# Two adaptive-norm transformer layers on one core: layer 1's modulation and residual placed elsewhere, layer 0's gates applied at the combination, PE's mixture programs written out with constant waits

## The chip, the cores and the metric

The kernel runs on one core of one Trainium2 chip, as one launch. Its engines are called here as the profile calls them: PE (matmul, with PEld for its weight loads), DVE (vector), ACT (activation), POOL (GpSimd) and SP (which mostly issues transfers). The metric is device microseconds of the whole execution, lower is better. A span is the time from the first to the last instruction of the program in the profiled execution.

## The reference, cut to what matters

The input is x of 2 batches x 512 tokens x 256 channels. Each of two layers does attention and a mixture of experts, both with a modulated norm ahead and a gate at the residual:

```
mod = (silu(c) @ wmod).reshape(2, 6, 1, 256)
sa, ca, ga, sb, cb, gb = (mod[:, i] for i in range(6))
ga, gb = [(2 * (g >= 0) - 1) * maximum(abs(g), 0.25) for g in (ga, gb)]
h = layernorm(x) * (1 + ca) + sa
x = x + ga * attention(h)                  # 16 heads of 16, causal
h = layernorm(x) * (1 + cb) + sb
x = x + gb * mixture(h)
# layer 0: 8 experts, the best 2 by score, hidden 176
#   comb = softmax(top 2); y_e = silu(h @ w1_e + b1_e) @ w2_e + b2_e
#   mixture(h) = sum_e comb_e * y_e
# layer 1: 16 experts, the best 4, 2 x 256 hidden
#   t = h * rsqrt(mean(h * h) + eps) * norm_w; G = softmax(top 4)
#   a, b = min(even, 7), clip(odd, -7, 7) of (t @ w1_e + b1_e)
#   y_e = (a * sigmoid(1.702 * a) * (b + 1)) @ w2_e + b2_e
#   mixture(h) = h + sum_e G_e * y_e
```

## The kernel before, in words

All 1024 tokens stay in SBUF as 8 tiles of 128 (`x`, `tok`). Each engine has a program of its own (the functions under `nc.Block()`), written out by hand in order, and semaphores tie them together. What stands first in an engine's program goes first, so an instruction that waits holds up everything behind it on its engine.

**Routing.** Behind the second norm of a layer PE turns the tokens batch by batch (`turn_batch(l, 2, b)`, L1310 is its transposes) and multiplies them with the gate weights (L1510). DVE takes the best scores (L1110 to L1127), subtracts the largest (L1131), ACT takes the exponent (L787), and DVE makes the gates of it (L1134 to L1136). PE counts with triangular and all-one matrices which token stands where among an expert's tokens (L1520 to L1527). DVE works out each token's slot and, per tile, tables of zeros and ones (L1177, L1181, L1185); ACT multiplies one of them with the gates (L798). With these tables PE places token numbers and weights into slots of 128 (L1535, `placed_ps`). DVE reads the token list (L1196 to L1199) and the expert of each slot tile, kept in `te` (L1200 to L1203).

**Layer 1's modulation** is computed within layer 0: PE makes its columns (L1285, `modulation_columns(1)`) and its rows (L1296, `modulation_rows(1)`) behind the gate matmuls of both batches. ACT copies the rows out (`move_modulation`, L700), DVE shapes them after the token list.

**Mixture.** Layer 0 has 23 slot tiles, layer 1 has 47. POOL gathers a tile's tokens from DRAM (L635). PE goes in steps: step s transposes tile s (`pe_x`, L1549), loads two expert numbers from `te` into registers (`experts_of`), does the first expert layer of tile s-1 (`pe_h`: bias L1564, weights L1567), transposes the hidden values of s-2 (`pe_hT`, L1576) and does the second layer of s-3 (`pe_y`: bias L1585, weights L1588). On PE, ACT and DVE the first 7 steps and the last 3 are written out; those between are a loop of four steps (`Fori`, `UNROLL`), whose waits compare semaphores with registers. ACT scales each result by its slot's weight while it evicts it (L836). Layer 0 stores the results to DRAM, and POOL gathers each token's two results back (L665, 16 gathers, with the inverse root of layer 1's first norm, L570, put in between them). Layer 1 adds them into DRAM rows (L644).

**Combination and residual.** `combine(l, b)` adds the two results of a pair of tiles (L926), multiplies by the modulation gate (L927) and adds to x (L929). For layer 0 it runs once behind the mixture (first batch) and once within layer 1 behind the first attention fills (second batch). In layer 1 the token itself is part of the mixture's result: POOL multiplies `tok` by the gate and adds it to x (L625, L629), behind the second norm, while DVE does the routing.

Of the kernel before, what the change touches and what calls it, by code (L numbers as in the profile page):

```python
# [10 lines left out]
P = 128  # L11
D = 256
KD = D // P
B = 2
S = 512
T = B * S
NT = T // P
# [48 lines left out]
def build_kernel(nc, dram, out):  # L66
    with ExitStack() as ctx:
# [140 lines left out]
        def weighed_tile(l):  # L208

            n = NT * TOPK[l]  # L210
            return at_tile[:, 0:n * 2 * MT[l]].rearrange("p (n a c) -> p n a c", n=n, a=2)
# [86 lines left out]
        h_added = sem("h_added")  # L298
# [261 lines left out]
        def _(pool):  # L560
# [12 lines left out]
            for l in range(2):  # L573
# [98 lines left out]
        def _(act):  # L672
# [30 lines left out]
            for l in range(2):  # L703
# [80 lines left out]
                if l == 0:  # L784
                    move_modulation(1)
# [5 lines left out]
                act.wait_ge(gate_ready, l + 1)  # L791
                act.wait_ge(brows_ready, 48 * (l + 1))
                for t in range(NT):
                    act.wait_ge(tile_of, NT * l + t + 1)
# [36 lines left out]
                def act_y(ii, off):  # L831
                    i, r, rnd = tile_at(ii, off)
                    act.wait_ge(y_ps[l], i + 1)
                    if not (isinstance(i, int) and i < 4):
                        act.wait_ge((y_kept, y_summed)[l][r], 16 * rnd)
                    nc.scalar.activation(yt[:, r, :], ps[6 + off % 2][:, 0:D], ACT.Copy,  # L836
                                         scale=weight[:, bass.ds(i, 1)]).then_inc(y_sb[l], 1)
# [23 lines left out]
        def _(dve):  # L861
# [57 lines left out]
            def combine(l, b):  # L919

                for m in (2 * b, 2 * b + 1):
                    rng = slice(2 * m, 2 * m + 2)
                    dve.wait_ge((acc_loaded, sums_loaded)[l][m], 64 if l == 0 else 32)
                    if l == 1:
                        dve.wait_ge(h_added, b + 1)
                    link(nc.vector.tensor_tensor(acc_in[:, 0, rng, :], acc_in[:, 0, rng, :], acc_in[:, 1, rng, :], ALU.add))  # L926
# [5 lines left out]
            for l in range(2):  # L932
# [173 lines left out]
                for b in range(B):  # L1106
# [19 lines left out]
                    with nc.allow_low_precision(reason="zeros and ones"):  # L1126
# [9 lines left out]
                nc.vector.tensor_tensor(gate[:, :, 0:K], gk, grec[:, :].unsqueeze(2).broadcast_to([P, NT, K]),  # L1136
                                        ALU.mult).then_inc(gate_ready, 1)
# [18 lines left out]
                for b in range(B):  # L1156
# [16 lines left out]
                    if l == 0 and b == 1:  # L1173
                        count(nc.vector.tensor_copy(slot_u[:, :], slotf[:, 0:NT * K]))
# [541 lines left out]
```

## Time and profile before

| what | value |
|---|---|
| median of 3 runs (lowest to highest) | 662.5 us (659.71 to 666.78) |
| the profiled execution | 663.1 us |
| its span | 661.3 us |
| busy share of the span: PE, DVE, ACT, POOL | 78%, 54%, 37%, 36% |
| mean granted clock of PE | 0.88 |

The kernel's stages lie one behind the other in the span: layer 0's attention up to about 150 us, its routing to 190, its mixture to 262, then its combination, layer 1's attention from 283, its routing from 443 to 473, its mixture to 642 and the end. An engine's share of the whole span says little, as each stage has a limit of its own; one stage is read from its timeline. "Idle before" names the time an engine stood still ahead of an instruction and what released it; "issue" means that the engine waited for nothing that the profile shows but its own sequencer.

### The profile page before, as it was taken

What the parts mean: (1) busy time and instruction counts of PE and PEld (TensorE: products, weight loads), DVE (VectorE), ACT (ScalarE), POOL (GpSimd) and SP (SyncE); (2) the same over time, 40 slices, a digit from 0 to 9 for tenths busy, and PEclk for the clock granted to TensorE, in tenths of its full rate; (3) what the DMA queues carried; (4) which work ended last, traced back from release to release, by engine and by line L of the source; (5) the groups of instructions that cost most, each with busy time, mean ns of one, the idle gap of its engine ahead of it and who ended that gap; (6) DMA issues with size and microseconds to landing.
All of it is one profiled execution on the core that took longest, in us unless ns stands there. A gap on an engine that the chain in (4) does not pass through costs nothing.

```text
span 661.3 us, 10115 instructions
## 1 busy us (share of the span) xinstructions
PE 515.3 (78%) x3124; PEld 336.8 (51%) x3125; DVE 355.3 (54%) x832; ACT 247.3 (37%) x546; POOL 239.0 (36%) x236
## 2 busy tenths in 40 slices
PE   3978889977759997073989898743599999999960
PEld 3444446546447775042545454533556666666640
DVE  3539777446452332347686863577544444444425
ACT  1425546642122322040256546422334444444430
POOL 2213130010033320733121700064247777777650
PEclk9989989998757999576999989965789999999995
DMA  8588160352035331328863633380125444444445
GB/s 284 79 102 106 34 128 5 134 235 82 0 97 168 104 96 56 95 61 106 129 88 51 176 129 131 141 308 2 32 49 81 79 79 79 79 75 80 67 42 196
DMA packets 34858, 67.21 MB, mean 102 GB/s; under 512 B 6628, under 2 KB 27572, under 8 KB 33928
## 3 DMA queue, kind: packets, MB, share of 16 engines
q0 software_dynamic: 14496, 31.08, 26.5%
q1 hardware_dynamic: 20040, 35.64, 17.7%
q8 instruction: 21, 0.34, 0.2%
q14 instruction: 13, 0.11, 0.1%
q10 hardware_dynamic: 288, 0.05, 0.0%
HBM read 38.92 MB, written 14.96 MB: 81 GB/s over the span
## 4 chain that ended last, share of the span: by engine, by line
PE 63%; DVE 14%; DMA 10%; ACT 4%; issue 4%; POOL 4%; SPq 0%; POOLq 0%; DVEq 0%; ACTq 0%
PE bank L1567 15%; PE bank L1588 9%; PE bank L1437 5%; PE bank L1407 4%; PE bank L1387 4%; DVE mx L1029 4%; DMA big<-parts 3%; PE bank L1549 3%; DMA big<-mT 3%; PE bank L1564 2%; PE bank L1576 2%; PE bank L1535 2%; PE bank L1363 2%; POOL ptm L665 2%; PE bank L1310 2%
## 5 line engine op out<-in xcount | busy, mean ns | idle before, releaser
L1029 DVE TENSOR_REDUCE mx<-bank 128x4 f32<-128x512 f32 (+2 forms) x96 | 98.0, 1041 | 39.2 <-PE bank L1390 38.7
L761 ACT ACTIVATE ptm<-bank 128x512 f32<-128x512 f32 x160 | 92.4, 597 | 58.5 <-PE bank L1410 55.8
L1567 PE MATMUL bank<-big,ptm 128*128 x280 | 112.0, 524 | 0.0
L635 POOL DMA_INDIRECT ptm<-token_rows,token x70 | 69.0, 985 | 101.6 <-DVE token L1199 51.3
L644 POOL DMA_INDIRECT sums<-ptm,token x47 | 74.4, 1584 | 31.1 <-ACT ptm L836 29.6
L430 POOL DMA_DIRECT2D big<-parts x72 | 38.8, 546 | 119.0 <-DVE parts L958 58.4
L1387 PE MATMUL bank<-big 96*128 96x128 bf16 (+3 forms) x256 | 64.0, 316 | 22.6 <-DMA big<-parts 15.8
L1407 PE MATMUL bank<-big 98*128 98x128 bf16 (+3 forms) x256 | 67.7, 309 | 11.0 <-DMA big<-mT 6.3
L1588 PE MATMUL bank<-big,ptm 128*128 (+1 forms) x280 | 73.0, 382 | 0.0
L1241 DVE TENSOR_SCALAR tok<-bank 128x256 f32<-128x256 f32 x47 | 20.0, 425 | 85.2 <-PE bank L1567 85.2
L1567 PEld LDWEIGHTS bank<-big,ptm 128*128 128x128 f32 x280 | 51.6, 198 | 26.3 <-issue 23.5
L1390 PE MATMUL bank<-constb 128*128 128x128 bf16 x256 | 52.5, 231 | 0.0
L820 ACT ACTIVATE ctxden<-tok 128x256 f32<-128x256 f32 x47 | 19.6, 417 | 87.8 <-DVE tok L1241 87.8
L1588 PEld LDWEIGHTS bank<-big,ptm 128*128 128x128 f32 (+1 forms) x280 | 48.1, 192 | 4.9
L1410 PE MATMUL bank<-constb 128*128 128x128 bf16 x256 | 49.0, 224 | 0.0
L570 POOL TENSOR_TENSOR rstd<-vareps,neghalf 128x4 f32<-128x4 f32 x8 | 8.6, 1077 | 108.9 <-DVE vareps L906 108.9
L1407 PEld LDWEIGHTS bank<-big 98*128 98x128 bf16 x256 | 25.5, 100 | 42.0 <-ACT ptm L761 17.7
L1387 PEld LDWEIGHTS bank<-big 96*128 96x128 bf16 x256 | 26.5, 104 | 39.3 <-issue 28.7
L836 ACT ACTIVATE ptm<-bank,weight 128x256 f32<-128x256 f32 x70 | 33.2, 475 | 28.2 <-PE bank L1588 24.6
L1437 PE MATMUL bank<-ptm,big 128*32 128x128 f32 (+3 forms) x512 | 41.9, 447 | 1.4 <-ACT ptm L761 1.4
L1549 PE MATMUL bank<-consts,ptm 128*128 128x128 f32 x140 | 29.0, 291 | 11.9 <-DMA ptm<-token_rows,token 11.9
L1310 PE MATMUL bank<-consts,tok 128*128 128x128 f32 x80 | 14.2, 336 | 28.5 <-DVE tok L915 24.2
(173 smaller groups left out, 835.2 us busy)
## 6 DMA issues: line engine op xcount, KB each, us to landing
big<-parts POOLq DMA_DIRECT2D x72, 128.0 KB, 5.9
big<-in_moe_dram SPq DMA_DIRECT2D x1, 6144.0 KB, 19.4
big<-in_moe_dram POOLq DMA_DIRECT2D x1, 4096.0 KB, 15.3
big<-in_moe_dram SPq DMA_DIRECT2D x1, 3456.0 KB, 11.3
big<-parts SPq DMA_DIRECT2D x24, 128.0 KB, 5.6
results<-ptm SPq DMA_DIRECT2D x23, 128.0 KB, 1.7
sums<-zeros SPq DMA_DIRECT2D x2, 1152.0 KB, 7.6
modbc<-modulation_rows SPq DMA_DIRECT2D x2, 1024.0 KB, 9.7
```

Of the source, the lines that this page charges most:

```text
L635: nc.gpsimd.indirect_dma_start(out=xt[:, i % 4, :], out_offset=None, in_=xs[l][:, :], in_offset=bass.IndirectOffsetOnAxis(ap=token[:, i:i ...
L644: nc.gpsimd.indirect_dma_start(out=acc[i % 2][:, :], out_offset=bass.IndirectOffsetOnAxis(ap=token[:, i:i + 1], axis=0), in_=yt[:, i % 4, ...
L761: nc.scalar.activation(dst, src, ACT.Exp).then_inc(b_exp[l], 1)
L1029: nc.vector.tensor_reduce(mx[:, g % 2, :].rearrange("p (j i) -> p j i", j=HG)[:, j0:j0 + n, i], a_view(c), AX.X, ALU.max).then_inc(a_max[l ...
L1387: nc.tensor.matmul(dst[:, j, :], qr[u][0:SROWS, hl, i * P:(i + 1) * P], kr[u][0:SROWS, hl, 0:w], start=True, stop=False)
L1390: last = nc.tensor.matmul(dst[:, j, w - P:w], ident_b, causal_b, start=False, stop=True)
L1407: nc.tensor.matmul(ps[4 + c % 2][:, col:col + S - k * P], kr[u][0:MROWS, hl, k * P:(k + 1) * P], qr[u][0:MROWS, hl, k * P:S], start=True, ...
L1410: last = nc.tensor.matmul(ps[4 + c % 2][:, col:col + P], causal_b, ident_b, start=False, stop=True)
L1437: last = nc.tensor.matmul(ps[6][32 * j:32 * j + 32, k * P:S], vaug[:, b * TB + k, hg * HG + j, :], pt[:, g % 2, j, PK[k]:PK[k] + S - k * P ...
L1549: last = nc.tensor.transpose(ps[off % 2][:, k * P:(k + 1) * P], xt[:, r, k * P:(k + 1) * P], ident)
L1567: last = nc.tensor.matmul(dst, xtT[:, off % 2, k, :], moe_w1(l, k, e), start=False, stop=(k == KD - 1))
L1588: last = nc.tensor.matmul(dst, hidT[0:HK[l], off % 2, k, :], moe_w2(l, k, e), start=False, stop=(k == 1))
```

## The change

Seven things are edited.

- PE makes the columns of layer 1's modulation between the gate matmuls of the two batches, and its rows behind the ranking, ahead of the placing.
- ACT takes layer 0's exponent ahead of copying those rows out.
- In layer 0 the gates no longer go through the placing: ACT's weighing (L798) is gone there, PE places 24 columns instead of 48, ACT evicts results unscaled, and `combine` multiplies each result by its token's gate on DVE.
- DVE makes layer 0's tables with one operation a batch instead of one a tile.
- Layer 1's gate times token and its addition to x go from POOL to DVE, behind the expert numbers and ahead of the first tile.
- PE's mixture programs have no loop: all 26 and 50 steps are written out with constant waits.
- The load of the expert numbers has no check of its range.

The diff, cut to its core:

```diff
@@ gpsimd @@
-                if l == 1:
-                    pool.wait_ge(tok_ready[1], B)
-                    for b in range(B):
-                        rng = slice(b * TB, (b + 1) * TB)
-                        nc.gpsimd.tensor_tensor(tok[:, rng, :], tok[:, rng, :],
-                                                modbc[:, b, 3, :].unsqueeze(1).broadcast_to([P, TB, D]),
-                                                ALU.mult).then_inc(pool_own, 1)
-                        pool.wait_ge(pool_own, 3 + b)
-                        nc.gpsimd.tensor_tensor(x[:, rng, :], x[:, rng, :], tok[:, rng, :], ALU.add).then_inc(h_added, 1)
@@ scalar @@
+                act.wait_ge(gexp_in, l + 1)
+                nc.scalar.activation(gexp[:, :, 0:TOPK[l]], gexp[:, :, 0:TOPK[l]], ACT.Exp).then_inc(gexp_done, 1)
                 if l == 0:
                     move_modulation(1)
-                act.wait_ge(gexp_in, l + 1)
-                nc.scalar.activation(gexp[:, :, 0:TOPK[l]], gexp[:, :, 0:TOPK[l]], ACT.Exp).then_inc(gexp_done, 1)
...
-                for t in range(NT):
-                    act.wait_ge(tile_of, NT * l + t + 1)
+                for t in range(NT if l == 1 else 0):
+                    act.wait_ge(tile_of, t + 1)
...
+                    scale = weight[:, bass.ds(i, 1)] if l == 1 else 1.0
+                    nc.scalar.activation(yt[:, r, :], ps[6 + off % 2][:, 0:D], ACT.Copy, scale=scale).then_inc(y_sb[l], 1)
@@ vector, combine @@
+                    if l == 0:
+                        for t in (2 * m, 2 * m + 1):
+                            count(nc.vector.tensor_scalar(acc_in[:, 0, t, :], acc_in[:, 0, t, :], gate[:, t, 0:1], None, ALU.mult))
+                        settle()
+                        for t in (2 * m, 2 * m + 1):
+                            count(nc.vector.scalar_tensor_tensor(acc_in[:, 0, t, :], acc_in[:, 1, t, :], gate[:, t, 1:2],
+                                                                 acc_in[:, 0, t, :], ALU.mult, ALU.add))
+                        settle()
+                    else:
+                        link(nc.vector.tensor_tensor(acc_in[:, 0, rng, :], acc_in[:, 0, rng, :], acc_in[:, 1, rng, :], ALU.add))
@@ vector, tables of layer 0 @@
+                        link(nc.vector.tensor_tensor(
+                            marks, first[:, c].unsqueeze(2).broadcast_to([P, TB * K, MT[0]]),
+                            iota_t128[:, 0:MT[0]].unsqueeze(1).broadcast_to([P, TB * K, MT[0]]), ALU.is_equal))
+                        count(nc.vector.tensor_tensor(
+                            weighed_tile(0)[:, c, 0, :].rearrange("p (t k) c -> p t (k c)", t=TB),
+                            marks.rearrange("p (t k) c -> p t (k c)", t=TB),
+                            left[:, rng].unsqueeze(2).broadcast_to([P, TB, K * MT[0]]), ALU.mult))
+                        nc.vector.tensor_tensor(
+                            at_p[:, c, :], place[:, c].unsqueeze(2).broadcast_to([P, TB * K, P]),
+                            iota_p.unsqueeze(1).broadcast_to([P, TB * K, P]), ALU.is_equal).then_inc(place_of, TB)
@@ vector, ahead of layer 1's mixture @@
-                    dve.wait_ge(h_added, B)
+                    for b in range(B):
+                        rng = slice(b * TB, (b + 1) * TB)
+                        link(nc.vector.tensor_tensor(tok[:, rng, :], tok[:, rng, :],
+                                                     modbc[:, b, 3, :].unsqueeze(1).broadcast_to([P, TB, D]), ALU.mult))
+                        count(nc.vector.tensor_tensor(x[:, rng, :], x[:, rng, :], tok[:, rng, :], ALU.add))
+                    settle()
@@ tensor, routing @@
-                if l == 0:
-                    pe.wait_ge(wo_read[0], NT // 2)
-                    modulation_columns(1)
-                    modulation_rows(1)
+                    if (l, b) == (0, 0):
+                        modulation_columns(1)
...
                 last.then_inc(rank_ps, 1)
+                if l == 0:
+                    pe.wait_ge(wo_read[0], NT // 2)
+                    modulation_rows(1)
@@ tensor, mixture @@
                     _, pair = nc.values_load_multi_w_load_instructions(
-                        te[0:1, bass.ds(s, 1), :].rearrange("p a b -> p (a b)"), engines=[mybir.EngineType.PE],
-                        min_val=0, max_val=E - 1)
+                        te[0:1, s, :], engines=[mybir.EngineType.PE], min_val=0, max_val=EXPERTS[l] - 1,
+                        skip_runtime_bounds_check_because="a sum of zeros and ones, held to at most the last expert")
...
-                for s in range(STEADY):
-                    pe_step(0, s)
-                with pe.Fori(0, (SLOTS_T[l] - STEADY) // UNROLL) as ii:
-                    for q in range(UNROLL):
-                        pe_step(ii, STEADY + q)
-                for s in range(SLOTS_T[l], SLOTS_T[l] + 3):
+                for s in range(SLOTS_T[l] + 3):
                     pe_step(0, s)
```

PE's program in layer 0's routing, in order, before (`gw` are the gate weights, `silc` the modulation's input, `chosen` the ranking's):

```order
L1510 MATMUL bank<-gw,feat 128x8 x8
L1310 MATMUL bank<-consts,tok 128x128 x8
L1510 MATMUL bank<-gw,feat 128x8 x8
L1285 MATMUL bank<-silc,big 128x2 x8
L1296 MATMUL bank<-big,silc 2x512 x4
L1520 MATMUL bank<-chosen,constb 128x64
```

The same place in the program of the change, its beginning:

```order
L1531 MATMUL bank<-gw,feat 128x8 x8
L1306 MATMUL bank<-silc,big 128x2 x8
L1331 MATMUL bank<-consts,tok 128x128 x8
L1531 MATMUL bank<-gw,feat 128x8 x8
L1538 MATMUL bank<-chosen,constb 128x64
```

The columns (128x2) have gone between the batches' gate matmuls, and the ranking follows the second batch directly. From the ranking's last counts to the placing (L1559) the change has:

```order
L1541 MATMUL bank<-chosen,ones_b 128x16
L1541 MATMUL bank<-chosen,ones_b 128x8
L1545 MATMUL bank<-chosen,ones_b 128x8 x8
L1317 MATMUL bank<-big,silc 2x512 x4
L1559 MATMUL bank<-parts,ptm 128x24 x16
```

The rows (2x512) now stand behind the ranking and ahead of the placing.

PE's program in layer 0's mixture, the end of the loop before, from a tile's transposes on (the ISA rows behind the load are the check of its range; the others set an expert's address):

```order
L1549 MATMUL bank<-consts,ptm 128x128 x2
L1554 ISA
L1554 TENSOR_LOAD te
L1554 ISA x4
L1564 ISA
L1564 MATMUL bank<-ptm,ones_b 128x176
L1567 ISA
L1567 MATMUL bank<-big,ptm 128x176
```

A step's registers are set around its load. The loop's last step ends so, and the written-out end of the mixture begins behind it:

```order
L1588 ISA
L1588 MATMUL bank<-big,ptm 128x256
L1614 REGISTER_ALU
L1614 COMPARE_AND_BRANCH
L1554 TENSOR_LOAD te
```

The counter and the branch close each round of four steps. The same step in the change, where it stands once for each tile:

```order
L1573 MATMUL bank<-consts,ptm 128x128 x2
L1578 TENSOR_LOAD te
L1588 ISA
L1588 MATMUL bank<-ptm,ones_b 128x176
L1591 ISA
L1591 MATMUL bank<-big,ptm 128x176
```

The load stays; the address computed ahead of it, the four instructions of the check, the counter and the branch are gone.

DVE's program in layer 0's first combination, its second pair of tiles and the statistics behind it, before:

```order
L926 TENSOR_TENSOR ptm<-ptm 128x512
L927 TENSOR_TENSOR ptm<-ptm,modbc 128x512
L929 TENSOR_TENSOR x<-x,ptm 128x512
L900 BN_STATS stats<-x 128x6 x4
L903 BN_AGGR mv<-stats 128x2 x4
```

One addition opens the pair. In the change:

```order
L915 TENSOR_SCALAR ptm<-ptm,gate 128x256 x2
L918 SCALAR_TENSOR_TENSOR ptm<-ptm,gate 128x256 x2
L923 TENSOR_TENSOR ptm<-ptm,modbc 128x512
L925 TENSOR_TENSOR x<-x,ptm 128x512
L889 BN_STATS stats<-x 128x6 x4
L892 BN_AGGR mv<-stats 128x2 x4
```

Where one addition stood, two scalings and two scale-and-adds of a tile each stand now.

## Rows read from the trace of the kernel before

**Rows 1.** The page: its head.

```profile
span 661.3 us, 10115 instructions
```

**Rows 2.** Windows: length, busy by engine (instructions), granted clock, DMA share, GB/s.

```profile
520.00:560.00 40.00, 40.00 (x168) 25.37 (x167) 19.09 (x49) 17.11 (x49) 30.78 (x25) 1.00 0.48 78
```

**Rows 3.** Timeline of layer 0's routing: start, us, engine, line, operation [idle before <-releaser].

```profile
160.51 1.97 PE L1310 MATMUL bank<-consts,tok 128*128 128x128 f32 x8 [2.69 <-DVEq L1020]
...
166.60 3.55 PE L1285 MATMUL bank<-silc,big 128*128 128x2 f32 x16
...
168.93 0.17 DVE L1131 TENSOR_TENSOR gexp<-top 128x16 f32<-128x16 f32 x1
...
170.08 5.32 PE L1296 MATMUL bank<-big,silc 128*2 128x512 f32 x8
...
176.64 0.17 DVE L1134 TENSOR_REDUCE gsum<-gexp 128x8 f32<-128x16 f32 x1 [7.55 <-ACT gexp L787]
...
180.77 7.39 PE L1535 MATMUL bank<-parts,ptm 128*128 128x48 f32 x32 [4.88 <-ACT parts L798]
...
189.90 1.11 POOL L635 DMA_INDIRECT ptm<-token_rows,token  x1 [31.61 <-DVE token L1199]
```

**Rows 4.** Windows inside layer 0's routing, columns as in rows 2.

```profile
170.00:175.00 5.00, 5.00 (x9) 0.83 (x9) 0.00 (x0) 0.00 (x0) 0.00 (x0) 0.64 0.00 0
...
181.00:184.00 3.00, 3.00 (x16) 3.00 (x16) 2.79 (x16) 1.32 (x6) 0.00 (x0) 0.50 0.00 0
```

**Rows 5.** Timeline of PE, a tile's first transposes in layer 0's mixture.

```profile
211.70 0.38 PE L1549 MATMUL bank<-consts,ptm 128*128 128x128 f32 x2
...
215.95 0.38 PE L1549 MATMUL bank<-consts,ptm 128*128 128x128 f32 x2
...
252.80 0.38 PE L1549 MATMUL bank<-consts,ptm 128*128 128x128 f32 x2
```

**Rows 6.** Waits of PE, 195 to 262 us: us in total, times, longest.

```profile
PE bank L1564 <- issue: 6.1, 10, 1.8
```

**Rows 7.** Timeline around layer 0's two combinations.

```profile
279.83 0.17 DVE L906 TENSOR_SCALAR vareps<-mv 128x4 f32<-128x4 f32 x1
...
280.56 1.05 POOL L570 TENSOR_TENSOR rstd<-vareps,neghalf 128x4 f32<-128x4 f32 x1
...
307.95 1.42 DVE L915 TENSOR_SCALAR tok<-x,mv,rstd 128x256 f32<-128x256 f32 x4 [1.15 <-POOL rstd L570]
...
310.38 1.91 PE L1310 MATMUL bank<-consts,tok 128*128 128x128 f32 x8
```

**Rows 8.** Groups of instructions: busy us, mean ns, idle before.

```profile
L1006 DVE SCALAR_TENSOR_TENSOR tok<-tok,rstd,modbc 128x256 f32<-128x256 f32 x16 | 6.7, 479 | 0.2
...
L926 DVE TENSOR_TENSOR ptm<-ptm 128x512 f32<-128x512 f32 x8 | 5.5, 691 | 27.5 <-DMA ptm<-results,slot_u 14.8 <-DMA ptm<-sums 12.6
```

**Rows 9.** Timeline: the same cast in layer 0 and in layer 1.

```profile
162.16 0.17 DVE L1122 CAST idf<-idx 128x8 f32<-128x8 uint32 x1
...
450.78 2.34 POOL L629 TENSOR_TENSOR x<-x,tok 128x1024 f32<-128x1024 f32 x1
...
451.03 2.12 DVE L1122 CAST idf<-idx 128x16 f32<-128x16 uint32 x1
```

**Rows 10.** Timeline of the start of layer 1's mixture.

```profile
473.01 0.39 DVE L1203 CAST te<-tef 1x47 int32<-1x47 f32 x2
...
479.01 0.60 PE L1564 MATMUL bank<-ptm,ones_b 96*128 x1 [0.64 <-issue]
...
483.13 0.42 DVE L1241 TENSOR_SCALAR tok<-bank 128x256 f32<-128x256 f32 x1 [9.73 <-PE bank L1567]
```

**Rows 11.** Timeline of POOL's gathers for layer 0's combination.

```profile
271.54 1.17 POOL L665 DMA_INDIRECT ptm<-results,slot_u  x1 [0.30 <-issue]
...
273.01 0.95 POOL L665 DMA_INDIRECT ptm<-results,slot_u  x1 [0.30 <-issue]
```

**Rows 12.** The page: queues that fetch instructions.

```profile
q8 instruction: 21, 0.34, 0.2%
```

More of the change, by code:

```diff
@@ L210, in weighed_tile @@
             n = NT * TOPK[l]
-            return at_tile[:, 0:n * 2 * MT[l]].rearrange("p (n a c) -> p n a c", n=n, a=2)
+            return at_tile[:, 0:n * (1 + l) * MT[l]].rearrange("p (n a c) -> p n a c", n=n, a=1 + l)
         acc_in = ptm[:, 0:2 * NT * D].rearrange("p (a t c) -> p a t c", a=2, t=NT)
@@ L790, in _ @@
                 K = TOPK[l]
-                act.wait_ge(gate_ready, l + 1)
-                act.wait_ge(brows_ready, 48 * (l + 1))
-                for t in range(NT):
-                    act.wait_ge(tile_of, NT * l + t + 1)
+                if l == 0:
+                    move_modulation(1)
+                else:
+                    act.wait_ge(gate_ready, 1)
+                    act.wait_ge(brows_ready, 48 * 2)
+                for t in range(NT if l == 1 else 0):
+                    act.wait_ge(tile_of, t + 1)
                     v = weighed_tile(l)
@@ L1135, in _ @@
                 link(nc.vector.reciprocal(grec[:, :], gsum[:, :]))
[L1136 to L1137 removed]
+                weigh = nc.vector.tensor_tensor(gate[:, :, 0:K], gk, grec[:, :].unsqueeze(2).broadcast_to([P, NT, K]),
+                                                ALU.mult)
+                if l == 1:
+                    weigh.then_inc(gate_ready, 1)
+                else:
+                    count(weigh)
                 dve.wait_ge(rank_ps, l + 1)
@@ L1529, in _ @@
                 last.then_inc(rank_ps, 1)
+                if l == 0:
+                    pe.wait_ge(wo_read[0], NT // 2)
+                    modulation_rows(1)
                 for t in range(NT):
                     pe.wait_ge(place_of, NT * l + t + 1)
-                    pe.wait_ge(tile_weighed, NT * l + t + 1)
+                    if l == 1:
+                        pe.wait_ge(tile_weighed, t + 1)
+                    w = (1 + l) * MT[l]
                     for n in range(t * K, (t + 1) * K):
-                        last = nc.tensor.matmul(ps[4][:, 0:2 * MT[l]], at_place[:, n * P:(n + 1) * P],
-                                                at_tile[:, n * 2 * MT[l]:(n + 1) * 2 * MT[l]],
+                        last = nc.tensor.matmul(ps[4][:, 0:w], at_place[:, n * P:(n + 1) * P],
+                                                at_tile[:, n * w:(n + 1) * w],
                                                 start=(n == 0), stop=(n == NT * K - 1))
@@ L1545, in pe_x @@
                     pe.wait_ge(xt_loaded[r], TILES_BEFORE[l][r] + 16 * rnd + 16)
-                    if not (isinstance(i, int) and i < 2):
+                    if i >= 2:
                         pe.wait_ge(xT_sb[l], i - 1)
@@ L1561, in pe_h @@
                     dst = ps[2 + off % 2][:, 0:HB[l]]
-                    if not (isinstance(i, int) and i < 2):
+                    if i >= 2:
                         pe.wait_ge(h_free, i - 1)
@@ L1572, in pe_hT @@
                     pe.wait_ge(hid_ready[l], i + 1)
-                    if not (isinstance(i, int) and i < 2):
+                    if i >= 2:
                         pe.wait_ge(hT_sb[l], i - 1)
@@ L1582, in pe_y @@
                     dst = ps[6 + off % 2][:, 0:D]
-                    if not (isinstance(i, int) and i < 2):
+                    if i >= 2:
                         pe.wait_ge(y_sb[l], i - 1)
```

31 lines of the change are left out of this document (15 added, 16 removed).

## The prediction

> **What bounds the kernel now.** The page comes first, for its span of 661.3 us [rows 1]; the execution took 663.1, so 1.8 lie outside the span. Windows by stage come next. They part the mixtures into two kinds. In layer 1's mixture PE is busy for 40.00 of 40.00 us at the full clock [rows 2]: what feeds PE faster there gives nothing back. Layer 0's routing is the opposite, and its timeline is to be read as a relay [rows 3]. DVE hands ACT the exponent's input at 168.93 and then waits 7.55 us for the answer. ACT stands in front of the copy of layer 1's modulation rows, and those are still being made on PE, which works on layer 1's columns (3.55 us) and rows (5.32 us) until 175.40. DVE resumes at 176.64, PE starts placing at 180.77 and is done at 188.16, and POOL's first gather issues at 189.90. No engine is at its limit in these 20 us; the order is.
>
> Then PE alone in layer 0's mixture. From 211.70 to 215.95, where steps are written out, two tiles take 4.25 us, 2.13 each, with PE busy throughout. From 215.95 to 252.80, the loop, 14 tiles take 36.85, 2.63 each [rows 5]. The waits put it on the first matmul that needs an expert's number: 6.1 us in 10 waits, released by "issue", so by PE's own sequencer [rows 6].
>
> **The change, part by part.**
>
> *Layer 0's routing.* Three edits act together. PE's columns of layer 1 go between the two batches, where PE waited 2.69 us for DVE before its transposes at 160.51 [rows 3]. The rows go behind the ranking. The exponent goes ahead of ACT's copies. ACT's eight-fold weighing disappears, since the gates are applied later.
> New relay: the exponent's input is there at 169.10; with ACT's 0.2 us and two hand-overs I put DVE's return at 169.4 (at worst the 1.24 us that lie between 175.40 and 176.64, and those still hold ACT's copies). The first batch's tables are ready 4.13 us after that return as before (180.77 minus 176.64), plus the difference between a whole batch's table and one tile's: at most two 512-column operations, 2 x 0.69 = 1.38 [rows 8]. That makes 174.9. PE ranks at about 169.1 to 170.0 and does the rows until 175.3, so the placing begins there and, at the old 7.39, ends at 182.7: 5.5 us earlier than 188.16. The upper bound is a placing at half that time. PE placed at a granted clock of 0.50, the 1.2 GHz level, after idling; the rows before it ran in a window of mean 0.64, so the clock rose to 2.4 GHz during them [rows 4], and the placing now follows them directly. At 3.7 us it would end at 179.0, 9.2 us earlier. The second batch's tables come some 3 us after the first's, so the whole cannot be had. **I take -7.0, of -5.5 to -9.2.** If the columns lost their cover, they would cost up to 3.55 less the 2.69.
>
> *PE's programs written out.* The loop's 14 tiles go from 2.63 to 2.13 each: 14 x 0.51 = 7.1, and the step behind the last one has the same stall, 0.5. The lower bound is 0, since the load of the expert's number stays; the check of its range (four instructions) and the counters go. 2.13 is PE's own work, so nothing lies beyond it. I take the written-out rate, since that row holds the load and the check too. **-7.6, of 0 to -7.6.** For the start of the mixture the load still stands between the first transposes and the first expert matmul; of the longest wait of 1.8 only the check goes, at a few tiles: **-1.5, of 0 to -3.** In layer 1 the pace is PE's: 0. Its start had one such wait, 0.64 [rows 10]: **-0.5.**
>
> *Gates at the combination.* A pair of tiles had three operations of 512 columns. It gets two scalings of 256 (1.42 / 4 = 0.36 each [rows 7]) and two scale-and-adds of 256 (0.48) for one addition (0.69) [rows 8]: 0.72 + 0.96 - 0.69 = +1.0. In the first combination only the second pair is late: its variance, done at 280.00, comes at 281.0, and POOL, which took it at 280.56 between gathers, starts 0.45 later. The second combination is 2.0 longer; its normalised rows were ready at 309.37 and PE took them at 310.38, so 1.0 shows. **+1.5, of +0.5 to +3.** ACT's evictions with a constant scale and the missing copy of the weights are put at 0; DVE's other work covers a tenth of a us.
>
> *Layer 1's modulation and residual.* POOL loses four operations. One of them, 450.78 to 453.12, ran across a cast on DVE that takes 0.17 in layer 0 and took 2.12 there, ending just behind it [rows 9]; DVE's routing hangs on that cast. **-1.9, of 0 to -1.95.** DVE gains four operations of 1024 columns, 4 x 1.38 = 5.5 at most, behind its last cast at 473.40: done at 478.9. Its first tile's work came at 483.13 [rows 10], so 4.2 us of cover are left. Behind them on DVE stand the first tile's limits, for which ACT and then PE wait; without the cover they cost 5.5. POOL's first gathers now run beside them: a gather beside DVE's additions took 1.17 against 0.95 [rows 11], +0.2 each, inside the 0.5 above.
> [...]
>
> *Sum:* -7.0 - 7.6 - 1.5 - 0.5 + 1.5 - 1.9 = -17.0. 663.1 - 17.0 = 646.1. This execution lies 0.6 above the median of the runs (662.5), so I say **645**.
>
> **The rivals.**
> *The register load holds the written-out pace too.* For it: the load stays in every tile, and the four steps that ran at 2.13 came after slow ones in which the sequencer could run ahead. Against it: those rows hold the load and a check besides. Without the 7.6: 653.
> *The residual on DVE holds up the first gathers of layer 1.* For it: the cast in rows 9. Against it: rows 11. Price: the four operations, 5.5, straight on PE's start: 650. Together with the first rival: 658.
> *The placing runs wholly at the full clock and the first tiles lose their waits.* -2.2 and -1.5 more: 641, and some lower.
> *Slower: PE's longer program starves PE.* PE's rows in the program's order grow from 1574 to 2235, and its instructions come through a queue, 21 packets so far [rows 12]; by the rows' ratio some 9 more (an estimate), nearly all inside the mixtures, where PE is the bound. From 1.9 us a packet the whole gain is gone; at 3 us it is 27 - 17 = +10: 672. Against it: the four written-out tiles in rows 5 show no such stall.
>
> **How the numbers follow.** Forecast as summed 0.60; the faster case 0.10; the first rival 0.14; the gathers alone 0.06; both 0.05; slower 0.05. A measurement of this kernel tells about 1% from no change, so 6.6 us. Faster by that (below 655.9): 0.60 + 0.10 + 0.06 + 0.11 of the first rival's 0.14, whose other terms may fall to their lower bounds: 0.87. Within 1%: 0.03 + 0.05 = 0.08. Slower: 0.05. The range runs from 637 (the faster case with the executions' own spread of some 3 us) to 653, and leaves out the double rival, the slow case and half of the first rival, below 2 in 10.
>
> **What would show it.** DVE's 7.55 us wait for the exponent gone, PE's layer 1 rows behind the ranking and directly ahead of the placing, the first gather near 183. First transposes 2.13 us apart through all of layer 0's mixture, and no "issue" total of 6.1 on the first expert matmul. Layer 1's mixture still 40.00 of 40.00 busy. The cast of rows 9 at 0.17. Scalings and scale-and-adds near 0.36 and 0.48, POOL's inverse root waiting for them about half a us. DVE's four operations ended before the first tile's limits. It is wrong if tiles of layer 0 still stand 2.6 us apart, if gathers at layer 1's start take 2 us, or if PE shows gaps spaced evenly through the mixtures.

## The result, and the profile after

The changed kernel takes 647.4 us (median of four runs, 645.5 to 649.8) against 664.6 of the kernel before, measured beside it (659.7 to 668.5): a ratio of 0.973, 95% interval 0.969 to 0.978. The forecast was 645, in a range of 637 to 653. The profiled execution of the changed kernel took 649.8 us, with a span of 648.0 against 661.3 [rows 1]. Two executions of the experiments below ran at a lower mean granted clock than the others of their kernels (0.86 and 0.78) and are left out of the times given: 646.6 us with the zeroing earlier, which expectations that go by 639.6 still count, and 690.2 with layer 1's rows behind the placing.

The page first: its head, and the queue that fetches instructions, to be read beside [rows 1, 12].

```profile
span 648.0 us, 9617 instructions
...
q8 instruction: 27, 0.44, 0.3%
```

The timeline of layer 0's routing is the answer to [rows 3] (start, us, engine, line, operation, and in brackets the idle time before it and what ended it).

```profile
161.66 2.05 PE L1306 MATMUL bank<-silc,big 128*128 128x2 f32 x16
...
164.49 1.97 PE L1331 MATMUL bank<-consts,tok 128*128 128x128 f32 x8 [0.78 <-DVEq L1016]
...
173.11 0.22 ACT L773 ACTIVATE gexp<-gexp 128x16 f32<-128x16 f32 x1 [6.01 <-DVE gexp L1127]
...
173.36 0.17 DVE L1130 TENSOR_REDUCE gsum<-gexp 128x8 f32<-128x16 f32 x1 [0.28 <-ACT gexp L773]
...
173.63 5.24 PE L1317 MATMUL bank<-big,silc 128*2 128x512 f32 x8
...
178.80 1.97 PE L1559 MATMUL bank<-parts,ptm 128*128 128x24 f32 x16
...
181.65 1.97 PE L1559 MATMUL bank<-parts,ptm 128*128 128x24 f32 x16 [0.89 <-DVE ptm L1186]
...
185.28 1.11 POOL L623 DMA_INDIRECT ptm<-token_rows,token  x1 [22.99 <-DVE token L1216]
```

The relay runs as the steps said: the columns lie where PE had waited for DVE, DVE waits 0.28 us and no longer 7.55 for the exponent, the rows follow the ranking, and the placing follows the rows. Windows (columns as in rows 2) of the rows, the placing, 14 tiles of layer 0's mixture and 40 us of layer 1's:

```profile
173.63:178.80 5.17, 5.17 (x12) 0.73 (x9) 4.67 (x18) 0.00 (x0) 0.00 (x0) 0.68 0.00 0
178.80:183.70 4.90, 3.93 (x33) 3.72 (x32) 3.03 (x10) 2.35 (x3) 0.00 (x0) 1.00 0.01 3
...
211.76:241.53 29.77, 29.77 (x197) 26.86 (x196) 11.84 (x28) 9.82 (x28) 10.42 (x11) 1.00 0.38 117
...
505.00:545.00 40.00, 40.00 (x169) 25.36 (x167) 19.28 (x48) 17.52 (x48) 30.77 (x25) 1.00 0.49 80
```

The placing has a granted clock of 1.00, the 2.4 GHz level, where it had 0.50 [rows 4]; the 14 tiles take 29.77 us of busy PE, 2.13 each, where they took 36.85 [rows 5]; layer 1's mixture has PE full as before [rows 2].

The table parts both profiled executions at the same events: the start of the first gate matmul (155.87 before, 159.85 after), of the first gather, of the ninth and the 23rd tile's transposes, the end of PE's last matmul of layer 0's mixture, and so on; each entry is the difference of two events in the trace.

| Stretch, us | before | after | difference | forecast |
|---|---|---|---|---|
| start to layer 0's first gate matmul | 155.87 | 159.85 | +4.0 | 0 |
| to the first gather (routing) | 34.04 | 25.42 | -8.6 | -7.0 |
| to the ninth tile's transposes | 26.05 | 26.48 | +0.4 | -1.5 |
| to the 23rd tile's | 36.85 | 29.77 | -7.1 | -7.6 with the next |
| to the end of layer 0's mixture | 8.18 | 6.37 | -1.8 | (in the line above) |
| to layer 1's first turned batch | 22.40 | 22.61 | +0.2 | +1.5 with the next |
| to the second turned batch | 27.01 | 28.72 | +1.7 | (in the line above) |
| to layer 1's first gate matmul | 124.30 | 125.22 | +0.9 | 0 |
| to its first gather | 38.09 | 36.08 | -2.0 | -1.9 |
| to its first expert matmul | 6.24 | 5.35 | -0.9 | -0.5 |
| to PE's end | 161.45 | 160.24 | -1.2 | 0 |
| to the end of the span | 20.82 | 21.89 | +1.1 | 0 |

The first line has nothing to do with the change: PE's program is the same up to there. In the 14 profiled executions of this study that stretch ends anywhere from 154.9 to 160.7, and its length goes with the granted clock: from 20 to 154 us that is 0.97 in the three that end by 156.0 (before is one) and 0.94 in the five that end behind 159.8 (after is one). One of the places is 67.70 to 74.60, with 0.51 after against 1.00 before.

Where the forecast missed is the start of layer 0's mixture. Its tiles on PE, after:

```profile
191.34 0.32 PE L1588 MATMUL bank<-ptm,ones_b 96*128 x1 [0.72 <-issue]
...
193.88 0.32 PE L1588 MATMUL bank<-ptm,ones_b 96*128 x1 [0.47 <-issue]
...
196.52 0.69 PE L1573 MATMUL bank<-consts,ptm 128*128 128x128 f32 x2 [0.57 <-DMA ptm<-token_rows,token]
...
198.48 0.32 PE L1588 MATMUL bank<-ptm,ones_b 96*128 x1 [1.27 <-issue]
```

The waits for the expert's number are still there in the first tiles, and the fourth tile's gather lands late. What moves data just then is SP's zeroing of the two sums of layer 1, 1152 KB each, issued behind layer 1's modulation rows:

```profile
189.04 1.43 SPq L470 DMA_DIRECT2D sums<-zeros  x2
```

### The profile page after: what moved, and what is told of

It reads as the page before. It is cut to its first block, busy times and chain, and to the rows that moved or that the text cites. A ratio compares the mean times of both kernels' runs of the same rounds, so it can differ in the third digit from the quotient of the medians.

```text
span 648.0 us, 9617 instructions
## 1 busy us (share of the span) xinstructions
PE 512.5 (79%) x3124; PEld 334.2 (52%) x3124; DVE 359.4 (55%) x829; ACT 241.8 (37%) x530; POOL 229.5 (35%) x232
## 4 chain that ended last, share of the span: by engine, by line
PE 62%; DVE 15%; DMA 9%; issue 4%; ACT 4%; POOL 3%; SPq 0%; POOLq 0%; DVEq 0%; ACTq 0%
PE bank L1591 15%; PE bank L1612 9%; PE bank L1458 6%; PE bank L1428 5%; PE bank L1408 4%; DVE mx L1025 4%; DMA big<-mT 3%; PE bank L1384 3%; PE bank L1573 2%; PE bank L1600 2%; PE bank L1588 2%; PE bank L1559 2%; PE bank L1346 2%; PE bank L1331 2%; PE bank L1411 2%
## 5 line engine op out<-in xcount | busy, mean ns | idle before, releaser
L1408 PEld LDWEIGHTS bank<-big 96*128 96x128 bf16 x256 | 26.8, 105 | 38.0 <-issue 27.4
L1458 PE MATMUL bank<-ptm,big 128*32 128x128 f32 (+3 forms) x512 | 44.1, 464 | 1.4 <-ACT ptm L749 1.4
L1384 PE MATMUL bank<-feat,wqkv 128*128 128x512 f32 x64 | 35.1, 692 | 2.0 <-ACT feat L679 2.0
## 6 DMA issues: line engine op xcount, KB each, us to landing
big<-in_moe_dram SPq DMA_DIRECT2D x1, 6144.0 KB, 19.7
big<-in_moe_dram SPq DMA_DIRECT2D x1, 3456.0 KB, 11.1
```

The lines of the kernel that those rows point to most:

```text
L1384: last = nc.tensor.matmul(fill_bank(n), wqkv[:, k, lo:lo + P], feat[:, k, b * S:(b + 1) * S], start=(k == 0), stop=(k == KD - 1))
L1408: nc.tensor.matmul(dst[:, j, :], qr[u][0:SROWS, hl, i * P:(i + 1) * P], kr[u][0:SROWS, hl, 0:w], start=True, stop=False)
L1458: last = nc.tensor.matmul(ps[6][32 * j:32 * j + 32, k * P:S], vaug[:, b * TB + k, hg * HG + j, :], pt[:, g % 2, j, PK[k]:PK[k] + S - k * P ...
```

## The experiments

The edits are made to the changed kernel unless the text says otherwise; times are medians of four runs where no other number is given, and ratios are to runs of the kernel before beside them (medians 664.7 to 665.5). The changed kernel was not run again beside them.

### PE's programs back in the loop

```
- for s in range(SLOTS_T[l] + 3): pe_step(0, s)
+ for s in range(STEADY): pe_step(0, s)
+ with pe.Fori(0, (SLOTS_T[l] - STEADY) // UNROLL) as ii: ...
+ for s in range(SLOTS_T[l], SLOTS_T[l] + 3): pe_step(0, s)
```

> The changed kernel with PE's mixture programs put back into the loop (expert number checked, counters and waits against registers); all else as changed. If the loop's sequencer work was the whole cause of the 2.63 us per tile, 14 tiles of layer 0 go back from 2.13 to 2.63 us and the steps behind the last one slow down too: 647.4 + 8.9 (the two stretches read in the traces, 7.1 and 1.8) = about 656. If another part of the change made the pace (the eviction with a constant scale, the missing weights), it stays at 647 with 2.13 per tile. Layer 1's mixture should not move by more than 1.2 us.

Measured: 655.6 us (654.2 to 658.2), ratio 0.987 (0.983 to 0.991). The 14 tiles take 36.22 us again, 2.59 each, the end of the mixture 8.01. In their window PE is busy for 33.67 us of the 36.22, at the full clock:

```profile
208.71:244.93 36.22, 33.67 (x198) 27.22 (x197) 11.83 (x28) 9.82 (x28) 10.35 (x11) 1.00 0.30 95
```

Layer 1 loses 0.6 up to its first expert matmul and 1.2 behind it. The loop, with the check that stands in it, holds the pace, and no other part of the change does; the next run parts the two.

### Written out, with the check of the expert's number

```
  te[0:1, s, :], engines=[mybir.EngineType.PE], min_val=0, max_val=EXPERTS[l] - 1,
- skip_runtime_bounds_check_because="...")
+ )
```

> The changed kernel with PE written out, but with the check of the expert number's range kept in every step. If the check was what the loop lost its time on, layer 0's tiles are near 2.6 us apart and the time is near 655. If the loop's counters, register waits and branch were it, tiles stay 2.13 apart, only the first tiles' waits of 0.72, 0.47 and 1.27 us grow, and the time is 647 to 649. Both may be needed together: then the check alone fits beside PE's work, as does the loop alone, and the time is also near 648.

Measured: 653.1 us (650.6 to 654.6), ratio 0.982 (0.977 to 0.987). Neither expectation: the time is near the first one, the tiles are a mixture of both. The timeline of PE at the first transposes of four tiles:

```profile
210.50 0.38 PE L1573 MATMUL bank<-consts,ptm 128*128 128x128 f32 x2
212.62 0.38 PE L1573 MATMUL bank<-consts,ptm 128*128 128x128 f32 x2
...
240.58 0.38 PE L1573 MATMUL bank<-consts,ptm 128*128 128x128 f32 x2
243.08 0.39 PE L1573 MATMUL bank<-consts,ptm 128*128 128x128 f32 x2
```

The tiles start at 2.13 and stay there for seven distances; one of 2.20 follows, and then they come 2.36 to 2.50 us apart to the end. I read this as a lead of PE's sequencer, gathered while PE waited for its first tiles and then spent; behind that its own pace, 2.4 us a tile with the check, is what counts. The loop adds the rest up to 2.6: in its trace most distances are 2.37 to 2.55 too, but one in four is 2.98, once in each round of the loop.

### PE written out alone, in the kernel before

In the kernel before:

```
- for s in range(STEADY): pe_step(0, s)
- with pe.Fori(0, (SLOTS_T[l] - STEADY) // UNROLL) as ii: ...
+ for s in range(SLOTS_T[l] + 3): pe_step(0, s)   # no check, constant waits
```

> The kernel before with only PE's mixture programs written out. If the parts of the change are independent it gains the 8.9 us read in the traces: 664.6 - 8.9 = about 655.7, with tiles 2.13 apart. If the gain needs the other parts (ACT's scale read from memory by a register index holds the eviction and so PE), tiles stay above 2.13 and it gains less than 4.

Measured: 652.1 us (647.7 to 654.7), ratio 0.982 (0.976 to 0.987), so a gain of 8.5 to 15.7: the expected 8.9 lies inside, near its lower end. The 14 tiles take 29.77 and the end 6.37, the same as in the whole change: the part stands by itself. Its start of the mixture took 23.45 where before and after have 26.05 and 26.48; in this execution the granted clock was 0.50 for 11.1 us behind the first gather and not for 17.8 (before) or 19.0 (after). Windows (columns as in rows 2) of that time, of the kernel before and of this one:

```profile
189.90:207.70 17.80, 10.25 (x35) 7.77 (x36) 5.61 (x15) 1.22 (x4) 8.26 (x8) 0.50 0.60 200
```

```profile
190.12:201.20 11.08, 5.30 (x18) 3.73 (x18) 4.34 (x12) 0.43 (x2) 7.31 (x7) 0.50 0.69 228
```

Up to the ninth tile PE idles here for 7.0 us, as long as after the change (7.0) and nearly as long as before (7.6): with equal gaps the clock rose at different times.

### The zeroing issued earlier

```
  nc.sync.dma_start(wo[:, :, :], dram["wo"][1]).then_inc(ld_wo[1], 16)
- keep_rows(1)
  zero_sums(1)
+ keep_rows(1)
```

> The changed kernel with SP issuing the zeroing of layer 1's sums (2 x 1152 KB and 128 KB) ahead of keeping layer 1's modulation rows, so at about 165 us in the routing and not at 189 beside the first gathers. If these transfers are what made the third gather late and the waits in front of the first expert matmuls long (0.57 <-DMA, 0.72, 0.47, 1.27 <-issue), most of these 3.0 us go: 647.4 - 2 = about 645, the range 644.4 to 646.4, and the stretch from the first gather to the ninth tile's transposes falls from 26.5 to 23.5 to 25.5. If the load of the expert's number is slow by itself, the waits stay and so does the time, 647.4 within 1.

Measured: 639.1 us (635.6 to 640.0, three runs), ratio 0.958 (0.953 to 0.964). That is 8.3 below the changed kernel, where 2 were expected. SP now issues the zeroing in the routing:

```profile
163.70 2.17 SPq L470 DMA_DIRECT2D sums<-zeros  x2
```

From the first gather to the ninth tile it takes 19.58 us in place of 26.48. The waits of PE in layer 0's mixture (what waits, for what, us in total, times, longest), first of the changed kernel, then of this one:

```profile
PE bank L1573 <- DMA ptm<-token_rows,token: 6.2, 3, 4.7
PE bank L1588 <- issue: 2.5, 3, 1.3
```

```profile
PE bank L1573 <- DMA ptm<-token_rows,token: 5.7, 2, 4.7
PE bank L1588 <- issue: 0.2, 1, 0.2
```

The waits account for 2.8 of the 6.9 us. The rest is the clock: windows from the first gather to the rise of the granted clock and on to the ninth tile (columns as in rows 2), of the changed kernel and of this one.

```profile
185.30:204.30 19.00, 11.99 (x41) 9.02 (x42) 6.04 (x16) 1.34 (x4) 9.20 (x9) 0.50 0.58 194
204.30:211.76 7.46, 7.46 (x50) 6.68 (x48) 2.96 (x7) 2.42 (x7) 2.84 (x3) 1.00 0.35 107
```

```profile
182.54:191.20 8.66, 4.44 (x16) 3.55 (x17) 4.35 (x12) 0.32 (x1) 6.83 (x7) 0.50 0.28 80
191.20:202.12 10.92, 10.92 (x74) 9.85 (x73) 4.55 (x11) 3.44 (x10) 5.21 (x6) 1.00 0.39 119
```

PE was at the full clock 8.7 us after the first gather and not 19.0; the same matmuls that take 4.44 + 10.92 = 15.4 us of PE here took 19.5 there. The expectation counted the waits alone and was too small by that. How much of the clock's part belongs to the zeroing varies, as the clock rose at 11.1 us once with the zeroing in its old place (the run above). Over all traces the effect is clear: with the zeroing in its old place the stretch to the ninth tile takes 23.45 to 26.86 us (ten traces), with it issued earlier 19.58 to 21.72 (four).

### The zeroing earlier, with the check kept

```
- keep_rows(1); zero_sums(1)
+ zero_sums(1); keep_rows(1)
- skip_runtime_bounds_check_because="..."
```

> The changed kernel with the zeroing issued in the routing and the check of the expert number's range kept. It measures what the check costs in the first tiles once nothing crowds them. If the missing gain at the start (forecast 1.5 us) was there and only covered by the transfers, the stretch from the first gather to the ninth tile goes from 19.6 to 21 or 22, and the time is 639.6 + 5.7 + 1.5 to 2 = about 647. If the check has no price there, the stretch stays at 19.6 to 19.9 and the time is about 645.

Measured: 646.8 us (645.8 to 649.3), ratio 0.974 (0.970 to 0.978). From the first gather, at 183.10, to the ninth tile it takes 21.72, against 19.58 without the check:

```profile
204.82 0.38 PE L1573 MATMUL bank<-consts,ptm 128*128 128x128 f32 x2
```

The check costs 2.1 us there once the transfers are out of the way; with them in the way one pair of traces shows 0.3 (26.76 against 26.48). The gain that the forecast saw at the start exists; the transfers covered it.

### The zeroing earlier, in the kernel before

```
- keep_rows(1); zero_sums(1)
+ zero_sums(1); keep_rows(1)
```

> The kernel before with the zeroing alone issued earlier (near 161 us in place of 193). If the transfers crowd the first tiles whatever the change, the stretch from the first gather to the ninth tile falls from 26.05 to about 22 (eight tiles at the loop's 2.63 and the first tile's way), 664.6 - 4 = about 660.5. If they do harm only since the change made the gathers start earlier, it stays at 26 and the time at 664.6.

Measured: 662.2 us (657.5 to 665.9, ten runs), ratio 0.996 (0.993 to 0.999). The stretch falls from 26.05 to 21.34, so the crowding was there before the change. Of these 4.7 us the runs show 2.5; the two profiled executions differ by 5.6. The routing, beside which the zeroing now runs, takes 0.8 longer in this trace (34.79); why the rest does not show is open. The longest wait for the expert's number goes from 1.8 us [rows 6] to 0.6:

```profile
PE bank L1564 <- issue: 3.4, 9, 0.6
```

### The old order in layer 0's routing

```
- if (l, b) == (0, 0): modulation_columns(1)   # between the gate matmuls of the two batches
+ if l == 0: modulation_columns(1); modulation_rows(1)   # behind them, ahead of the ranking
  ...
+ if l == 0: move_modulation(1)   # ACT, ahead of the exponent
```

> The changed kernel with layer 1's columns and rows both put back on PE between the second batch's gate matmuls and the ranking, and with ACT's exponent back behind its copies; the whole-batch tables, the narrow placing and the missing weighing stay. If the order was what the routing gained by, the stretch from the first gate matmul to the first gather goes from 25.4 back to 32 to 34 us: 647.4 + 7 to 8.6 = 654 to 656. If ACT's weighing and the wide tables were the greater part, it stays below 29 and the time below 651.

Measured: 655.6 us (653.2 to 657.9), ratio 0.984 (0.981 to 0.988). The routing takes 34.13 us, what it took before (34.04). The whole gain of the routing needs the order: with the old one, the missing weighing and the whole-batch tables give nothing. What these two give with the new order was not run. DVE waits for the exponent as in rows 3, and PE places at half the pace again:

```profile
181.01 0.17 DVE L1130 TENSOR_REDUCE gsum<-gexp 128x8 f32<-128x16 f32 x1 [7.14 <-ACT gexp L775]
...
186.09 7.03 PE L1557 MATMUL bank<-parts,ptm 128*128 128x24 f32 x32 [5.83 <-DVE ptm L1186]
```

### Layer 1's rows behind the placing

```
- if l == 0: modulation_rows(1)
  for t in range(NT): ...   # the placing
+ if l == 0: modulation_rows(1)
```

> The changed kernel with layer 1's rows on PE behind the placing in place of ahead of it, so that PE idles between the ranking (ending near 173.7 us) and the first batch's table (ready at 178.4). If the rows in front are what makes the placing run at the full clock (1.97 us for a batch), the two batches take near 3.9 us each, the placing ends some 2.5 to 4 us later and the stretch to the first gather grows from 25.4 to 28 or 29. If the clock does not hang on them, the placing starts 0.4 earlier and the stretch stays at 25.4 or a little less, since the second batch's table is what it waits for. In both cases the rows then stand in front of layer 0's first tiles: 5.3 us of PE, part of it in the 3 us that PE waits for the first gather, so 2 to 8 us in the next stretch. Time 650 to 657 by the first, 648 to 653 by the second.

Measured: 647.9 us (647.9 to 649.8, three runs), ratio 0.974 (0.970 to 0.978): unchanged in sum. The routing grows by 1.9 us to 27.28. The placing, and the windows ahead of it and of it:

```profile
179.16 7.02 PE L1554 MATMUL bank<-parts,ptm 128*128 128x24 f32 x32 [4.74 <-DVE ptm L1186]
```

```profile
173.70:179.10 5.40, 0.66 (x16) 0.57 (x16) 4.64 (x20) 0.22 (x1) 0.00 (x0) 0.50 0.00 0
179.16:186.10 6.94, 6.94 (x32) 6.90 (x32) 3.33 (x12) 0.00 (x0) 0.00 (x0) 0.50 0.01 2
```

PE idles for 4.74 us ahead of it and its clock stays at 0.50; the 32 matmuls then take 7.02 us, against 2 x 1.97 behind the rows. So the rows in front give the placing its clock. The 2 to 8 us expected behind it didn't come: the rows fill the wait for the first gather, and the stretch to the ninth tile is 25.22.

### Layer 1's residual back on POOL

```
+ pool: tok = tok * modbc; x = x + tok   (for both batches, before layer 1's gathers)
- dve:  the same four operations
+ dve.wait_ge(h_added, B)
```

> The changed kernel with layer 1's modulation and residual back on POOL. If the 1.95 us of the cast is what the move gave, the cast takes 2.1 us again, the stretch from layer 1's gate matmuls to its first gather goes from 36.1 back to 38.1, and the stretch behind it stays at 5.4 or loses the 0.2 a gather that DVE's additions may cost: 647.4 + 2 = 649.4, of 649 to 650. If the move gave nothing, the stretch stays and so does the time.

Measured: 650.2 us (649.2 to 650.4), ratio 0.977 (0.974 to 0.980), 2.8 above the changed kernel by the medians, whose intervals overlap; the traces carry the reading. The stretch from layer 1's gate matmuls to its gather is 38.03 against 36.08. The cast on DVE is held by POOL's last operation as in rows 9:

```profile
440.43 2.13 DVE L1130 CAST idf<-idx 128x16 f32<-128x16 uint32 x1
```

```profile
440.19 2.34 POOL L629 TENSOR_TENSOR x<-x,tok 128x1024 f32<-128x1024 f32 x1
```

Behind the gather the stretch is 5.28 against 5.35, so DVE's additions beside the gathers cost 0.1 at most.

### The combination without its gates, and with ACT's help

```
- if l == 0: two scalings by gate[:, t, 0:1], two scale-and-adds by gate[:, t, 1:2]
- else:
+ if True:
      acc_in[:, 0, rng] = acc_in[:, 0, rng] + acc_in[:, 1, rng]
```

> The changed kernel with layer 0's two results added without their gates (the weighting is left out of the computation), so that the combination has its old three operations. It measures the price of the gates at the combination: by the traces 0.3 to 0.5 before layer 1's first turn and 1.7 before its second, so 647.4 - 2.1 = 645.3, the first stretch 19.2 to 19.4 and the second 27.0. If the attention hides the second, only 0.4 shows: 647.0.

Measured: 644.4 us (643.3 to 645.4), ratio 0.969 (0.966 to 0.973). The first stretch is 19.42 us from the first combination gather (19.66 with gates), the second 27.32 (28.72): 1.6 together by the traces, 3.0 by the medians, whose intervals overlap.

In the next one ACT multiplies by the first gate:

```
+ act: for m in range(4): wait acc_loaded[m]; acc_in[:, 0, t] = acc_in[:, 0, t] * gate[:, t, 0]
- dve: the same products
+ dve.wait_ge(scaled, 2 * m + 2)
```

> The changed kernel with ACT doing the combination's first scaling (its eight products by the first gate), so that DVE keeps the scale-and-adds. The second combination is DVE's: its two pairs lose 0.84 us each, the stretch between layer 1's first and second turned batch goes from 28.7 to about 27.0. In the first combination ACT's scaling stands in the same chain, so the stretch from the first combination gather to the turn stays at 19.7 or loses up to 0.5. 647.4 - 1.7 = 645.7, of 645.2 to 647. Rival: DVE is not what the second batch waits for (the attention hides it), so the time stays at 647.4 though the turn comes earlier.

Measured: 643.9 us (642.1 to 649.5), ratio 0.971 (0.965 to 0.977), not to be told from the changed kernel. The stretch to the second turned batch did not fall to 27.0, it grew to 30.22. ACT works in order, and its last scaling waits for the last gathers; the features of layer 1's first batch stand behind it, and PE waits 4.50 us for them:

```profile
268.39 0.91 ACT L851 ACTIVATE ptm<-ptm,gate 128x256 f32<-128x256 f32 x2 [6.05 <-DMA ptm<-results,slot_u]
```

```profile
270.78 9.30 PE L1388 MATMUL bank<-feat,wqkv 128*128 128x512 f32 x16 [4.50 <-ACT feat L680]
```

### Both improvements

```
- keep_rows(1); zero_sums(1)
+ zero_sums(1); keep_rows(1)
+ act: scale pairs 0, 1; move_transposed(1, 0, [0]); scale pairs 2, 3
```

> Both improvements together: the zeroing issued in the routing, and ACT doing the first scaling of the combination, the second batch's behind the features of layer 1's first batch (in the run before they stood ahead of them, waited for the last gathers until 268.39 us and made PE wait 4.50 us). From the first turned batch of layer 1 to the second it should be 28.7 - 1.2 (two scalings of 0.61 on DVE) = 27.5, the stretch from the first gather to the ninth tile 19.6 as with the zeroing alone, the time 639.6 - 1.2 = about 638.4, of 637 to 640. If the second batch's turn is hidden behind the scores, it is 639.6.

Measured: 639.0 us (637.8 to 641.1), ratio 0.961 (0.957 to 0.965). The stretch to the second turned batch is 27.37, as expected, but the time is that of the zeroing alone (639.1). This is the fastest version of the study, 8 us below the changed kernel, and the zeroing gives nearly all of it.

## Why the prediction was right, and where it was not

**Layer 0's routing**, -7.0 of -5.5 to -9.2: right in mechanism, 1.6 too small; the trace has -8.6, and the old order gives all of it back. The placing began where the steps put it, directly behind the rows. The term mis-sized is the placing: I kept most of the 7.39 us at half clock and named the full clock as the bound. It ran wholly at the full clock, 1.97 us a batch, with a wait of 0.89 for the second batch's table between; with PE idle in front instead of the rows, both took 7.02. That is the first half of the faster rival; its other half, the first tiles' waits, did not go.

**PE written out**, -7.6: it was -8.9, and the 1.3 more lie behind the 23rd tile's transposes, where the last four steps became 1.8 shorter together and I counted one at 0.5. But the reasoning behind the pace was weaker than its number. I took 2.13 us as the written-out rate because "that row holds the load and the check too". The trace before did not show such a rate. The last of its short distances, 213.83 to 215.95, starts at the eighth tile, and with seven steps written out that is the loop's first:

```profile
213.83 0.38 PE L1549 MATMUL bank<-consts,ptm 128*128 128x128 f32 x2
```

So the loop ran at 2.13 too at first. With the check kept, written-out steps hold 2.13 for seven distances and then need 2.4: the tiles of rows 5 ran on the sequencer's lead, as the first rival said. The rival was right on that row and wrong on the outcome, since without the check the load alone stays below 2.13.

**The start of layer 0's mixture**, -1.5 of 0 to -3: it was +0.4, the step that failed. It took the check to be what the waits were made of. They were made of two things. The check costs 2.1 us there, shown with the zeroing out of the way. The zeroing, 2.3 MB beside the first gathers, lengthened the waits for the gathers and for the expert's number, and the clock rose later beside it; it did so before the change too. What it slows in PE's sequencer is not shown: the waits are put down to "issue" and go when the transfers do, but no run parts the load of the expert's number from the fetch of PE's instructions. Nor do the runs show that the gaps delay the clock, since with the same total of gaps it once rose 8 us sooner.

**Layer 1**: the start, -0.5, was -0.9, and 0.6 comes back with the loop or the check alone. The pace is PE's, as said. The 1.2 us that layer 1 gained behind its first expert matmul also come back with the loop or the check (161.44 and 161.40 against 160.24); I had them at 0.

**Gates at the combination**, +1.5: the traces of the eight kernels with gates on DVE have 27.6 to 28.7 us between the turned batches, mean 28.3; the three of the old combination and the one without gates 26.8 to 27.3, mean 27.1. With 0.3 from the first combination (19.66 against 19.34 from its first gather) that is +1.5.

**Layer 1's residual**, -1.9: -2.0, and back when undone. DVE's four operations took 1.23 each and ended 3.8 us before the first tile's limits, against 4.2 forecast. In this timeline they run beside POOL's gathers:

```profile
461.33 1.23 DVE L1231 TENSOR_TENSOR tok<-tok,modbc 128x1024 f32<-128x1024 f32 x1 [0.16 <-DVE te L1220]
...
462.40 1.01 POOL L623 DMA_INDIRECT ptm<-token_rows,token  x1 [0.76 <-issue]
...
464.97 0.95 POOL L623 DMA_INDIRECT ptm<-token_rows,token  x1 [0.30 <-issue]
...
470.02 0.42 DVE L1262 TENSOR_SCALAR tok<-bank 128x256 f32<-128x256 f32 x1 [3.79 <-PE bank L1591]
```

A gather takes 1.01 or 0.95 us, and 0.97 or 0.95 where the four operations are back on POOL, so the rival in which they are held (650) is out. The page "SBUF — State Buffer" of the Trainium skill, section "SBUF: two separate sides", says that POOL cannot write descriptors while DVE runs an operation in a two-port mode. An operation of DVE with two SBUF inputs, it says, holds the shared ports only against a POOL operation that reads SBUF, and whichever of the two engines starts first keeps them for its whole instruction. The four operations have two inputs, and the 0.95 us shows no gather held by them. The cast, with the residual back on POOL, agrees with the last point: it started 0.24 us behind POOL's addition, took 2.13 and ended 0.03 behind it.

**The slower rival**, instructions starving PE: 6 more packets, not 9, and PE busy for 29.77 of 29.77 and 40.00 of 40.00 us. Out.

**The sum**: the stretches that the change touches give -8.6 - 8.9 + 0.4 + 1.5 - 2.0 - 0.9 - 1.2 = -19.7; the medians say -17.2, with -15.0 to -20.6 from the interval. What makes the 2.5 us between the two is open. The forecast's -17.0 came out partly by luck, because its misses cancelled: 1.6, 1.3, 0.4 and 1.2 too little gain, 1.9 too much.

## What to carry to other kernels

A pace read from a few iterations behind a wait may be the sequencer's lead and not its rate: look for the pace of a long run of iterations, or take away what you think it costs. A wait put down to "issue" can have transfers behind it that no row names; before costing it by the instructions that stand there, look at what the DMA queues carry at that moment, above all work with time to spare, such as zeroing, that can be issued in a stretch where the queues are quiet. And work placed directly ahead of a short stage on PE can do more than fill idle time: the placing behind the rows ran at the full clock, 3.94 us against 7.02. Ask what the same work would fill elsewhere; here, put behind the placing, it filled the wait for the first gather, and the time stayed the same.

## What the runs showed of the hardware

- PE's waits ahead of the first matmul that needs a loaded expert number grow beside large transfers: 2.5 us in three tiles fell to 0.2 when 2.3 MB of zeroing was moved away. Whether the load itself or the fetch of instructions is slowed is open.
- The same 32 placing matmuls took 7.02 us at a granted clock of 0.50 after 4.74 us of idle PE and 3.94 at 1.00 behind 5.24 us of other matmuls.
- Unchanged code differs by up to 5.8 us between profiled executions (154.9 to 160.7 up to the first gate matmul), and its length goes with the granted clock (a mean of 0.97 from 20 to 154 us in the shortest three, 0.94 in the longest five). A difference of one pair of profiles ahead of the changed code belongs to no edit.
